# Layer 0's cross-attention computed transposed, in four row groups of 32, with its stages interleaved by a written list

## The reference, cut to what matters

```python
x = x + gate_a * (softmax(q k^T * scale) v @ W_proj + b_proj)      # self-attention, 512 x 512 for each head
q_c = ln(x) @ W_qc + b_qc                                          # 512 x 128
k_c, v_c = split(ln(context) @ W_kvc + b_kvc)                      # 77 x 128 each
x = x + softmax(q_c k_c^T * scale) v_c @ W_cproj + b_cproj         # cross-attention, 512 x 77 for each head
x = x + gate_m * (gelu(modulate(ln(x)) @ W_mlp1 + b) @ W_mlp2 + b) # MLP, 512 hidden
```

## Time and profile before

| what | value |
|---|---|
| median of 3 runs | 457.37 us (457.35, 457.37, 461.53) |
| the profiled execution | 461.02 us, of it a span of 459.3 us on the core |
| mean granted TensorE clock in it | 0.859 of full speed |

### The profile page before, as it was taken

How to read it: one execution, slowest core, us unless ns; L and a number is a source line. 1 busy time by engine, 2 the same in 40 slices (tenths; PEclk the granted TensorE clock), 3 DMA queues, 4 the chain that set the end, 5 groups by cost and what they waited for, 6 DMA issues and landing times.

```text
span 459.3 us, 8983 instructions
## 1 busy us (share of the span) xinstructions
PE 366.4 (80%) x3326; PEld 214.9 (47%) x3326; DVE 303.5 (66%) x1281; ACT 204.1 (44%) x304; POOL 109.4 (24%) x130
## 2 busy tenths in 40 slices
PE   0958899999989987899979798866585566675885
PEld 0746322323333155677646547643363344453454
DVE  4386976999897056667236544236979999995332
ACT  1141036666656935566532032433444455654411
POOL 8047200002510011001022400011443544443010
PEclk9977658999999998999989586977877777776989
DMA  7236031112000000000000000000000000000000
GB/s 211 59 112 185 24 123 53 52 55 87 3 1 2 0 1 1 1 2 1 1 0 2 6 2 6 4 3 1 1 3 0 1 2 1 1 1 1 1 24 24
DMA packets 10811, 12.16 MB, mean 26 GB/s; under 512 B 2378, under 2 KB 9103, under 8 KB 10767
## 3 DMA queue, kind: packets, MB, share of 16 engines
q1 hardware_dynamic: 10469, 11.55, 8.6%
q0 software_dynamic: 256, 0.01, 0.0%
q10 hardware_dynamic: 42, 0.01, 0.0%
HBM read 8.69 MB, written 2.62 MB: 25 GB/s over the span
## 4 chain that ended last, share of the span: by engine, by line
PE 55%; DVE 28%; ACT 8%; issue 5%; POOL 1%; DMA 1%; SPq 1%; ACTq 0%; DVEq 0%
PE psum L1350 6%; PE psum L1410 6%; PE psum L1378 5%; PE psum L1363 5%; DVE mx L1125 4%; DVE left L1180 4%; DVE left L1187 4%; PE psum L1511 4%; PE psum L1251 3%; PE psum L1393 3%; DVE top L1177 3%; PE psum L1421 3%; DVE top L1184 2%; PE psum L1433 2%; PE psum L1448 2%
## 5 line engine op out<-in xcount | busy, mean ns | idle before, releaser
L1125 DVE TENSOR_REDUCE mx<-psum 128x1 f32<-128x512 f32 x128 | 80.2, 680 | 11.2 <-PE psum L1350 11.1
L731 ACT ACTIVATE big<-psum 128x1024 f32<-128x1024 f32 x64 | 62.4, 1022 | 42.3 <-PE psum L1363 42.0
L1350 PE MATMUL psum<-KS,QS 72*128 72x512 bf16 x128 | 51.1, 431 | 5.3 <-DVE mx L1125 4.4
L1410 PE MATMUL psum<-kblk,qf 128*128 128x308 f32 x128 | 48.0, 508 | 1.1 <-DVE qf L1058 0.8
L1421 PE MATMUL psum<-ident,pr 128*77 128x128 f32 x256 | 39.3, 305 | 9.9 <-POOL pr L672 9.8
L561 POOL TENSOR_TENSOR rstd<-vareps,minus_half 128x4 f32<-128x4 f32 x12 | 12.2, 1018 | 143.5 <-DVE vareps L901 143.4
L1421 PEld LDWEIGHTS psum<-ident,pr 128*77 128x77 f32 x256 | 35.3, 171 | 18.1 <-POOL pr L672 13.3
L1363 PE MATMUL psum<-QS,KS 75*128 75x512 bf16 x128 | 40.4, 404 | 0.4
L672 POOL TENSOR_TENSOR pr<-pr,early 128x616 f32<-128x616 f32 x16 | 23.9, 1493 | 56.0 <-ACT early L841 38.8
L1378 PE MATMUL psum<-big,V 128*9 128x512 f32 x256 | 35.2, 623 | 0.5 <-ACT big L731 0.5
L1350 PEld LDWEIGHTS psum<-KS,QS 72*128 72x128 bf16 x128 | 12.0, 103 | 47.4 <-DVE mx L1125 24.6
(11 more groups left out here) (195 smaller groups left out, 663.3 us busy)
## 6 DMA issues: line engine op xcount, KB each, us to landing
QS<-scr_q SPq DMA_DIRECT2D x8, 288.0 KB
KS<-scr_k SPq DMA_DIRECT2D x8, 288.0 KB
scr_q<-qp SPq DMA_DIRECT2D x2, 384.0 KB, 2.7
scr_k<-kp SPq DMA_DIRECT2D x2, 384.0 KB, 3.3
early<-in_L_xcond_w_ada_dram SPq DMA_DIRECT2D x1, 576.0 KB, 7.2
wmlp<-in_L_xcond_W_mlp_dram SPq DMA_DIRECT2D x2, 256.0 KB, 3.2
scr_k<-kp SPq DMA_DIRECT2D x2, 256.0 KB, 3.5
wm<-in_L_xcond_w_m_dram SPq DMA_DIRECT2D x1, 512.0 KB, 4.4
```

The source lines that it names most:

```text
L731: freed(act.activation(pT[:, u % 2, 1024 * half:1024 * (half + 1)], ps, ACT.Exp), "sT", 0, u, half)
L1125: freed(dve.tensor_reduce(mx[:, n % 3, NT * hh + q:NT * hh + q + 1], ps, AX_X, ALU.max), "max", t, q)
L1350: filled(pe.matmul(ps, QS[b][0:ROWS, h, q * P:(q + 1) * P], KS[b][0:ROWS, h, :], start=True, stop=True), "max", j, q)
L1410: last = pe.matmul(ps[:, 512 * a:512 * a + HH // 2 * S], qf[:, b, i * P:(i + 1) * P], kb[:, c0:c0 + HH // 2 * S], start=True, stop=True)
```

## The change

Only layer 0's cross-attention is computed another way; the order of the work between the self-attention loop and layer 1's top-16 stage is rewritten.

- S^T in row groups: `cross_q` makes q in four spread copies (chunk c holds heads 4c to 4c+3, head j in rows 32j to 32j+7, zeros below, row 32j+8 free for the negated maximum), `kcF` is the spread k with a one in that row. `cross_sT(b, c)` is four matmuls of 32 rows x 77 columns against 512 queries, one in each row group, in two rooms; `exp_cross` is two exps of 77 x 1024; `cross_out` is four matmuls 77 x 9 against 512 in four column groups. There are 8 such units (b, c) in place of 16 halves. No weights are turned.
- Maxima: `dense_q` is the old q; `cross_maxima(b, i)` is four matmuls of 32 rows against `kown` (each row group's own four heads, 308 columns), each in its own room with one VectorE reduce; `cross_max_turn` and four small DMAs (`cross_max_rows`) put the negated maxima into q's free rows.
- The result (9 rows for each head, transposed) is turned by VectorE in blocks of 32 x 32 (`dve.transpose`), divided, and turned once more for each batch into `oT`; W_cproj's rows are loaded permuted, in four DMAs, to match.
- Batch 0's dense q, spread q and maxima go into the steps t = 32 to 35 of the self-attention loop. All else up to the top-16 stage follows `STAGES`, one list for all engines. In it S, V are cross units; o, p, l a self-attention output's turn, projection and norm; d, q, m, t dense q, spread q, maxima, their turn; P, L output projection and norm; h, M, N the MLP's first half, second half, norm; a, v, x, y layer 1's q and k, v, window maxima, their turn; E, F, G the windows' S, V, T. The digits are batch and part.
- `kblk` (built by GpSimd once for each layer) gives way to `kown` for both layers, so layer 1's `cross_scores` is two matmuls of 32 rows in different row groups in place of two of 128 rows.

```diff
+T_Q = T_OUT + 7
+T_M = T_Q + 1
...
+STAGES = """
+    S00 S01 o1 V00 p1 S02 V01 S03 V02 l1 V03 d1 q10 q11 m10 m11 P0 q12 q13 m12 m13 t1 L0 h00 h01 h02 h03 S10 M0 S11 V10 S12 V11
+    S13 N0 V12 a00 a01 V13 a02 a03 v0 P1 x00 x01 x02 x03 y0 L1 h10 h11 h12 h13 E0 E1 M1 F0 E2 F1 G0 E3 F2 G1 N1 F3 G2 a10 a11
+    G3 a12 a13 v1 x10 x11 x12 x13 y1 oT out E4 E5 F4 E6 lnT F5 G4 E7 qc G5
+    """.split()
+WINDOWS_LATE = {0: ("F6",), 1: ("F7", "G6"), 2: ("G7",)}
 NQ, HALF = 4, 256
...
+            if name == "wcproj":
+                for j in range(NQ):
+                    eng.dma_start(dst[QUAD * j:QUAD * (j + 1), :],
+                                  src.rearrange("(c j d) n -> j c d n", c=NQ, j=NQ)[j]).then_inc(s_w[name], 16)
+                return
...
+        def cross_max_rows(sp, b):
+            wait_read(sp, "mTc", b)
+            wait_read(sp, "qc", 0, b, NQ - 1)
+            for j in range(NQ):
+                sp.dma_start(qcF[QUAD * j + D:QUAD * j + DV, b, :, :].rearrange("o c (i t) -> o (c i) t", t=P),
+                             mneg[H * j:H * (j + 1), b, :]).then_inc(s_crow[b], 16)
...
+            def spread_cross():
+                for n, name in enumerate(("wqc0", "wkv0")):
+                    pool.wait_ge(s_w[name], 16)
+                    pool.memset(wcF[n][:, :, :, D:QUAD], 0.0).then_inc(s_wcF, 1)
+                    pool.tensor_copy(wcF[n][:, :, :, 0:D], W[name][:, 0:C].rearrange("p (c j d) -> p c j d", c=NQ, j=NQ))\
+                        .then_inc(s_wcF, 1)
...
+            def own_keys():
+                pool.wait_ge(s_mask4, 1)
+                for l2 in range(2):
+                    wait_read(pool, "kc", l2)
+                    pool.tensor_tensor(kown[:, l2, :, :, :], kcT[:, l2, :, :].unsqueeze(2).broadcast_to([P, B, G, S]),
+                                       mask4[:, :].unsqueeze(1).unsqueeze(3).broadcast_to([P, B, G, S]), ALU.mult)\
+                        .then_inc(s_kown, 1)
...
+            def exp_cross(b, c):
+                u = NQ * b + c
+                if u < 2:
+                    pv_done(act, UNITS - 2 + u)
+                else:
+                    wait_full(act, "pvx", (u - 2) // NQ, (u - 2) % NQ)
+                for half in range(2):
+                    ps = read_room(act, "sTc", b, c, half)
+                    freed(act.activation(pT[0:S, u % 2, 1024 * half:1024 * (half + 1)], ps[0:S, :], ACT.Exp),
+                          "sTc", b, c, half)
...
+            def cross_q_out(b, c):
+                r = VECS["L0_b_qc"]
+                if (b, c) == (0, 0):
...
+                ps = read_room(dve, "qc", 0, b, c)
+                freed(dve.tensor_scalar(qcF[:, b, c, :], ps, colsF[:, c, r:r + 1], SCALE, ALU.add, ALU.mult),
+                      "qc", 0, b, c)
+            def dense_q_out(b):
+                c = VECS["L0_b_qc"]
+                ps = read_room(dve, "qcd", b)
+                freed(dve.tensor_scalar(qf[:, b, :], ps, cols[:, c:c + 1], SCALE, ALU.add, ALU.mult), "qcd", b)
+            def cross_maxima(b, i):
+                for r in range(NQ):
+                    ps = read_room(dve, "cmax", b, i, r)
+                    freed(dve.tensor_reduce(mxw[:, b, :, r, i], ps[:, 0:G * S].rearrange("p (k s) -> p k s", s=S),
+                                            AX_X, ALU.max), "cmax", b, i, r)
+            def minus_cross_max(b):
+                ps = read_room(dve, "mTc", b)
+                freed(dve.tensor_scalar(mneg[:, b, :], ps[0:H * NT, 0:P], -1.0, None, ALU.mult), "mTc", b)
+            def cross_out(b, c):
+                u = NQ * b + c
+                ps = read_room(dve, "pvx", b, c)
+                freed(dve.transpose(turned[:, u % 2, :], ps), "pvx", b, c)
+                wait_read(dve, "pvx", b, c)
+                tv = turned[:, u % 2, :].rearrange("p (k e) -> p k e", e=QUAD)
+                r = rdenx[:, u % 2, :]
+                dve.reciprocal(r, tv[:, :, D]).then_inc(s_rdenx, 1)
+                dve.wait_ge(s_rdenx, u + 1)
+                dve.tensor_tensor(o[:, b, :, :].rearrange("p i n -> p (i n)").rearrange("p (k e) -> p k e", e=QUAD)
+                                  [:, :, D * c:D * (c + 1)], tv[:, :, 0:D],
+                                  r.unsqueeze(2).broadcast_to([P, N // QUAD, D]), ALU.mult).then_inc(s_onx[b], 1)
+                if c == NQ - 1:
+                    dve.wait_ge(s_onx[b], NQ)
...
+            def cross_q(b, c):
+                if (b, c) == (0, 0):
+                    pe.wait_ge(s_wcF, 2)
+                if c == 0:
...
+                ps = open_room(pe, "qc", 0, b, c)
+                filled(pe.matmul(ps, wcF[0][:, c, :, :].rearrange("p j e -> p (j e)"), hT[:, b, :],
+                                 start=True, stop=True), "qc", 0, b, c)
...
+            def cross_maxima(b, i):
+                if (b, i) == (0, 0):
+                    pe.wait_ge(s_kown, 1)
...
+                for r in range(NQ):
+                    ps = open_room(pe, "cmax", b, i, r)
+                    rows = slice(QUAD * r, QUAD * (r + 1))
+                    filled(pe.matmul(ps[:, 0:G * S], qf[rows, b, i * P:(i + 1) * P],
+                                     kown[rows, 0, b, :, :].rearrange("p k s -> p (k s)"), start=True, stop=True),
+                           "cmax", b, i, r)
...
+            def cross_sT(b, c):
+                if c == 0:
+                    for part in range(2):
+                        wait_read(pe, "kcF", part)
+                    wait_read(pe, "qc", 0, b, NQ - 1)
+                    pe.wait_ge(s_crow[b], 16 * NQ)
+                for half in range(2):
+                    ps = open_room(pe, "sTc", b, c, half)
+                    for t in range(2):
+                        rows = slice(QUAD * (2 * half + t), QUAD * (2 * half + t + 1))
+                        last = pe.matmul(ps[0:S, t * N:(t + 1) * N], kcF[rows, c, b, :], qcF[rows, b, c, :],
+                                         start=True, stop=True)
+                    filled(last, "sTc", b, c, half)
+            def cross_out(b, c):
+                u = NQ * b + c
+                if u == 0:
+                    wait_read(pe, "vc", 0)
+                ps = open_room(pe, "pvx", b, c)
+                for half in range(2):
+                    wait_read(pe, "sTc", b, c, half)
+                for j in range(NQ):
+                    last = pe.matmul(ps[QUAD * j:QUAD * j + DV, :], vc[:, 0, b, NQ * c + j, :],
+                                     pT[0:S, u % 2, j * N:(j + 1) * N], start=True, stop=True)
+                filled(last, "pvx", b, c)
             def v(layer, b):
                 w = W[f"wqkv{layer}"]
...
+            def cross_scores(e):
                 b, i = steps[e // 2]
                 if e % (2 * NT) == 0:
-                    wait_read(pe, "qc", layer, b)
-                    pe.wait_ge(s_kblk, B * layer + b + 1)
-                kb = kblk[:, b, :, :].rearrange("p h s -> p (h s)")
-                ps = open_room(pe, "sc", layer, e)
+                    wait_read(pe, "qc", 1, b)
+                    pe.wait_ge(s_kown, 2)
+                ps = open_room(pe, "sc", e)
                 for a in range(2):
-                    c0 = S * (HH * (e % 2) + HH // 2 * a)
-                    last = pe.matmul(ps[:, 512 * a:512 * a + HH // 2 * S], qf[:, b, i * P:(i + 1) * P],
-                                     kb[:, c0:c0 + HH // 2 * S], start=True, stop=True)
...
+            for part in range(2):
+                ps = open_room(pe, "kcF", part)
+                for c in (2 * part, 2 * part + 1):
+                    at = B * S * (c % 2)
+                    last = pe.matmul(ps[:, at:at + B * S], wcF[1][:, c, :, :].rearrange("p j e -> p (j e)"), ctxT[:, 0, :],
+                                     start=True, stop=True)
+                filled(last, "kcF", part)
```

More of the change, by code:

```diff
@@ L204, in rooms_in_turns @@
+    use("M", "oT", 3, 1)
+    use("M", "out", 4, 1)
+    use("M", "out", 5, 0)
+    use("M", "lnT", 5, 1)
+    for c in range(NC_):
+        use("X", "mlp", 1, 1, c)
+        use("W", "mlpb", 1, c)
+    use("M", "out", 5, 1)
     return turn
@@ L1225, in _ @@
+            for c in range(NC_):
+                gate_mul(0, c)
+            residual(4, 1)
+            ln_stats(5, 1)
+            ln_norm(5, 1)
+            residual(5, 0)
+            for c in range(NC_):
+                gate_mul(1, c)
+            residual(5, 1)
         @block.tensor
@@ new lines, in _ @@
+            for e in range(-1, HALVES + 3):
+                if e + 1 < HALVES:
+                    cross_scores(e + 1)
+                for item in WINDOWS_LATE.get(e, ()):
+                    window(item)
+                if 1 <= e <= HALVES:
+                    cross_turn(e - 1)
+                if e % 2 == 0 and 1 <= e // 2 <= B * NT:
+                    cross_pv(e // 2 - 1)
+                if e % 2 == 0 and e >= 4:
+                    pv_turn(e // 2 - 2, "pvc")
+                if e == ARRIVE["oT"]:
+                    o_turn(2, 1, "pvT", 1, B * NT - 1)
```

(15 more changed lines are left out.)

1180 lines of the change are left out of this document (608 added, 572 removed).

## The result

The changed kernel took 476.23 us, the median of 4 runs (475.03 to 478.60), against 457.36 for the one before (4 runs, 456.36 to 461.53). The ratio is 1.044, with a 95% interval of 1.040 to 1.049: slower by 4%, where I had forecast 440. Its profiled execution took 477.34, with a span of 474.9 and a mean granted clock of 0.791; before it was 461.02, 459.3 and 0.859.

A forecast was written before the change was run, and what follows sets the result against it. TensorE was taken to bound the 147.4 us middle, VectorE the top-16 stage. Loop end 176.4 plus a list of 94 + 18 + 6, say 119, put first scores at 295.4; 17.0 saved in total, so 440 us, range 427 to 456.

The forecast's parts named there:

- For the clock I add 6: List between loop and top-16 stage: 6 us added for lower clock, citing batch 1's q and k, 9.57 against 6.9.
- rival (4): List: clock stays at its lower level as more matmuls use 32 rows; middle at 150, time 471; chance 3%.
- TensorE's work in the list: List, at full clock: 34 us of new work plus 60 that stays, in sum 94.
- about 18 in all: List: waits from walking its items, listed as 7, 3, 2.5, 1.5, 3, 2.3, 1.5 and 3 us.
- V03, x00 or E4: Sign of being wrong through the list's item order: TensorE gaps of over 3 us ahead of these items.
- The loop: Steps 32 to 35 of self-attention: batch 0's spread q 3.4 and maxima 6.7 to 8.3 us, less slack: +10.
- Ahead of the loop: Before the first max_L0: kcF's four matmuls stand in front of it, +2.5 us, from 0 to 4.
- The first top-16 scores: Start of the top-16 stage: first half's 2.44 us at low clock is halved, 1.1 saved; later halves under VectorE.
- The weighed rules: S^T and V: four row tiles at 3.07 times one by one, sum 1 us more; mode-change drain already inside the price.
- (1): S^T: row groups don't run side by side, S 3.4 instead of 1.0; +22 us, 462; chance 7%.
- (2): List keeps the old waits: 130 us in place of 119, time 451, or 457 with further costs; chance 15%.
- (3): List: stagger works better, waits of 8 and no clock loss, 102 to 106 us, time 426; chance 12%.

The follow-up runs named there:

- e6: Changed kernel with layer 0's maxima and layer 1's scores contracting all 128 rows against block-wide keys: 469.96 us, 1.018 of the kernel before.
- e5: Changed kernel with the list unstaggered, batch 1's cross-attention behind batch 0's, then MLPs and projections, GpSimd's norms in that order: 486.77 us, 1.065 of the kernel before.
- e11: Kernel before with score matmuls contracting only 32 rows, in layer 0's cross-attention alone: median 464.28 us.
- e2: Kernel before with score matmuls of both layers' cross-attention contracting only the 32 rows that hold their keys: 465.38 us, 1.018 of the kernel before.
- e12: Changed kernel with layer 0's S^T on all 128 rows, against keys zero outside their row group: 485.60 us, 1.061 of the kernel before.
- e8: Changed kernel with useless 128-row matmuls filling TensorE's waits ahead of norm turns, max turns and window maxima: median 481.46 us.
- e3: Changed kernel without layer 0's cross-attention maxima, their dense q, reduces, turns and small DMAs: 451.09 us, 0.987 of the kernel before.
- e4: Changed kernel with kcF's four matmuls and evictions moved from ahead of the self-attention loop into its steps 5 and 6: 474.63 us, 1.030 of the kernel before.
- e10: Kernel before with layer 0's cross-attention exps straight from PSUM, without VectorE's reduce and maximum subtraction: 450.91 us, 0.9816 of the kernel before.

## Why the prediction was wrong

**The step that failed** is the one sentence "For the clock I add 6". The list lost 25.6 us to the lower clock, and the loop, for which the forecast has no clock term, 8.3 more than before's. Less the 6 that is 27.9 us, out of 32.6 by which the span missed. Behind the sentence stand two errors. I had called the 36 us between the old stages' 147.4 and their 111 of work waits, though 15.4 of them were clock, and a walk from item to item prices no clock. And of the windows with row tiles I let the one at 1.00 speak against rival (4) and used the one at 0.50 for 6 us only the earlier trace rows, though both show 32-row tiles. The outcome went the way of that rival, to which I gave 3%, not by its sum: 51 of 120 busy us were at the lower clock, not all.

Term by term, forecast against measured in the profiled execution:

- TensorE's work in the list: 94, measured 94.7. Units of S and V 1.0 each: 1.10 and 1.04, and 2.00 where a room waits for an exp.
- Waits in the list: "about 18 in all", measured 22.7. The eight waits that the prediction lists add up to 23.8, so their sum would have been nearly right, and they were added wrongly; with 23.8 the forecast would have been some 446. No wait of 3 us stood ahead of V03, x00 or E4; the longest was 2.57, at batch 1's norm. Most are small.
- Clock in the list: 6, measured 25.6. With 4.7 of waits, 0.7 of work and less the 1 that I had rounded up, the middle makes 24.0 of the 32.6 us by which the span missed the forecast.
- The loop: +10 (8 to 13), measured +16.8, of which 9.0 are work and 8.3 clock (S^T at 168.12 takes 1.89 us, at 154.42 it took 1.03). e6, without a low stretch behind the maxima, has +9.3 in all. So the work was priced rightly, and the clock not at all. (The prediction reads eight PV starts between 148.78 and 161.45; the trace has seven, and the 2.1 us a step is right.)
- Ahead of the loop: +2.5 (0 to 4), measured +3.6, of it 2.42 on kcF's matmuls at the lower clock; the average over all profiled executions is 2.5.
- The first top-16 scores: -1.1, their matmuls went from 2.44 us to 1.09 in the chain of after, and the rest is 0.4 shorter in all. VectorE is what it waits for there, as said.
- The block turn: taken at 0.7 between nothing and 1.4, measured 0.715.
- Reduces of 308 columns: 0.47 alone and 0.42 in a row, measured 0.476 mean, eight in 3.57 (0.45).
- Two more table loads of 1.28 and exps of 77 x 1024 at 1.02: 1.283 and 1.015. The two loads for GELU end 0.88 us before their input is there.

**The weighed rules.** A unit of four row tiles took 1.10 us and one after another 3.60, a factor of 3.3; the estimate that I had worked out from the Trainium skill, "TensorE: Matmul & The Clock Gate", Part 3, was 1.12, and the trace agrees within its error. The drain at a change of mode, which the Trainium skill states in "TensorEngine Tiling (Array Packing)", Key Properties, isn't seen as a gap: S^T at 191.28 ends as V begins at 192.31. If there is one, it is inside their 1.10 and 1.04 us, as the prediction took it.

**The rivals.** (1) is refuted by the unit's 1.10. (2), old waits kept, was near in size for the waits (22.7 against 21.3 of before) and priced at 451. (3) is half right: against the batches in turn the stagger saves 11.6 us of waits and 10.4 of clock in the middle (e5), but against the kernel before neither fell: waits 23.0 and 22.1, clock 25.8 and 17.1. (4) is above.

**What is shown and what is open.** Shown: the maxima cost 25 us of the change, 12 to 16.5 in the loop; with narrow score matmuls in a full stage the clock was lower in seven of eight executions and 5 us of gain (16 halves by 0.32) became 5 to 7 of loss (e11, e2); in the loop a low stretch stands behind the 32-row maxima and none behind full-row ones (e6); in the list neither the maxima's rows (e6) nor S^T's (e12) decide alone. Among the kernels with the list, the clock's cost goes with the idle time at either end, 15.7 at 14.8 (e8) and 36.2 at 34.6 (e5), but not between: e3 has 24.0 at 26.4, e12 27.8 at 21.1. Open: why the clock in the list fell more than in the old middle at nearly the same idle time (23.0 and 22.1). No run had every matmul of the list on 128 rows at once, and the V units have only 9 columns of weights in each column group in both kernels.

## What to carry to other kernels

Split a stage's time into work at full clock, time lost to the lower clock, and waits, before saying what a new order will remove; here 15 of the 37 us that I took for waits were clock, and an order that shortened the waits by 11.6 us moved the clock by 10.4 as well (e5 against after). An edit that makes matmuls narrower in a stage where TensorE is full must be costed at both clocks: 0.72 or 1.33 us against 1.04. Add up the listed terms once more before the sum is used: mine were 6 us short. And ask of each supporting step whether it is needed at all: subtracting the maximum cost 25 us in one kernel and 9 in the other, and dropping it is the larger gain; whether it may go depends on the range of the scores, not on the profile.

## What the runs showed of the hardware

- The mean clock differs between executions of one kernel, and the time follows it: before took 452.83 us at 0.875 and 462.41 at 0.859, e4 470.82 at 0.803 and 479.38 at 0.781, about 4 us for 0.01 in the latter. In the loop, with the same TensorE instructions, the time from the first max to the last PV was 119.1 to 122.6 in before, e2, e10 and e11, and 134.5 to 139.4 in after, e5, e8 and e12.
- A clock of 0.63 or 0.76 in the top-16 stage (after, e6) made no difference to its length, and yet moves the mean clock of the run: the mean says little without the stage.
- A 128x512 block turn of float32 took 0.715 us from PSUM and 0.712 in SBUF.
